# Six terms of a piecewise linear curve added up by GpSimd, ten by TensorE

## What is computed

```python
h = x @ w1 + b1                       # [3125, 1024] @ [1024, 512]
h = round(h * 256) / 256
y = interp(h, X, Y)                   # X: 33 knots from -4 to 4, Y: exact GELU there
y = where(h > 4, h, where(h < -4, 0, y))
y = round(y * 256) / 256
out = round((y @ w2 + b2) * 256) / 256
x = x + out                           # x is normalised before w1
```

## Time and profile before

| | |
|---|---|
| median of 3 runs | 3742.73 us (3742.1 to 3743.62) |
| the profiled execution, its own time | 3739.34 us |
| its span, first to last instruction | 3737.7 us |
| busy in the span: PE | 3444.8 us (92%) |
| busy in the span: DVE | 2799.8 us (75%) |
| busy in the span: ACT | 1582.1 us (42%) |
| busy in the span: POOL | 924.0 us (25%) |

### The profile page before, as it was taken

The page is one execution under the profiler, slowest core; times in us unless marked ns, Lnnn a source line. Parts: engine busy times, 40 slices in busy tenths (PEclk is TensorE's granted clock), DMA queues, the critical chain, the costliest instruction groups (busy, mean ns, idle before and its releaser), DMA issues. The chain is left out here.

```text
span 3737.7 us, 52878 instructions
## 1 busy us (share of the span) xinstructions
PE 3444.8 (92%) x17197; PEld 2842.2 (76%) x17197; DVE 2799.8 (75%) x6375; ACT 1582.1 (42%) x2646; POOL 924.0 (25%) x564
## 2 busy tenths in 40 slices
PE   6899999979999968991999999999999999699998
PEld 5678888658888847771888888888888888577776
DVE  4577677667777744333988989889889898688886
ACT  2011111121111102111777777777777777354454
POOL 1266671057766775660000000000000000000000
PEclk8999999989999989995999999999999999899999
DMA  7833322334444433323011110110110110322221
GB/s 264 350 50 66 66 51 65 104 90 89 89 88 88 88 76 75 47 43 106 23 45 39 28 45 25 42 45 22 45 45 23 45 37 14 112 74 82 82 71 50
DMA packets 234863, 269.87 MB, mean 72 GB/s; under 512 B 177236, under 2 KB 177236, under 8 KB 231642
## 3 DMA queue, kind: packets, MB, share of 16 engines
q1 hardware_dynamic: 57741, 216.14, 19.0%
q0 software_dynamic: 173776, 40.24, 7.5%
q10 hardware_dynamic: 3250, 12.50, 0.9%
HBM read 177.03 MB, written 90.75 MB: 72 GB/s over the span
## 5 line engine op out<-in xcount | busy, mean ns | idle before, releaser
L1194 PE MATMUL G_acc<-values,G_probsT 125*125 125x256 f32 x5000 | 1165.0, 380 | 0.0
L1194 PEld LDWEIGHTS G_acc<-values,G_probsT 125*125 125x125 f32 x5000 | 901.9, 188 | 113.8 <-ACT G_probsT L1057 0.3
L317 POOL DMA_INDIRECT counts<-E_twins_now,E_cells_now x400 | 859.6, 2149 | 389.9 <-issue 252.6
L1030 ACT ACTIVATE G_probs<-G_asrc_row,G_shift 125x625 f32<-125x625 f32 x500 | 409.0, 818 | 384.6 <-PE G_tr L1178 284.2
L1102 DVE TENSOR_TENSOR G_probs<-G_probs,G_low 125x625 f32<-125x625 f32 x500 | 402.3, 805 | 99.9 <-issue 66.0
L1178 PEld LDWEIGHTS G_tr<-ident,G_probs 125*125 125x125 f32 x2500 | 339.5, 189 | 180.2 <-DVE G_probs L1104 160.6
L1178 PE MATMUL G_tr<-ident,G_probs 125*125 125x125 f32 x2500 | 369.7, 279 | 108.1 <-DVE G_probs L1104 103.4
L1104 DVE SCALAR_TENSOR_TENSOR G_probs<-G_probs,G_count 125x625 f32<-125x625 f32 x500 | 405.2, 810 | 17.3
L1035 ACT ACTIVATE G_low<-G_asrc_row,G_low_shift 125x625 f32<-125x625 f32 x500 | 407.5, 815 | 22.9 <-DVE G_probs L1102 22.6
L218 PE MATMUL V_v_ps<-V_w,V_xT 128*125 128x512 f32 x1200 | 281.4, 397 | 43.7 <-DVE V_xT L242 43.7
L218 PEld LDWEIGHTS V_v_ps<-V_w,V_xT 128*125 128x125 f32 x1200 | 224.2, 187 | 100.9 <-DVE V_xT L242 44.1
(11 more groups left out here) (169 smaller groups left out, 3943.1 us busy)
## 6 DMA issues: line engine op xcount, KB each, us to landing
counts<-K_zeros POOLq DMA_DIRECT2D x50, 763.5 KB, 8.3
G_count<-counts SPq DMA_DIRECT2D x25, 1367.2 KB
xnT<-K_xT_whole SPq DMA_DIRECT2D x25, 500.0 KB
Q_xT_whole<-xnT SPq DMA_DIRECT2D x25, 500.0 KB
V_xT_whole<-xnT SPq DMA_DIRECT2D x25, 500.0 KB
E_row<-edge_keys ACTq DMA_DIRECT2D x25, 488.3 KB
E_row<-edge_keys SPq DMA_DIRECT2D x25, 488.3 KB
K_rows<-in_x SPq DMA_DIRECT2D x25, 448.0 KB
```

The source lines that it names most:

```text
L317: nc.gpsimd.indirect_dma_start(out=counts_cells, out_offset=bass.IndirectOffsetOnAxis(ap=self.cells_now[:, slot, c:c + 1], axis=0), in_=se ...
L1030: nc.scalar.activation(probs[:, u % 4, :], asrc_row[:, h, s:s + UW], ACT.Exp, bias=shift[:, sl, h:h + 1]).then_inc(high_ready, 1)
L1194: m = nc.tensor.matmul(acc[0:T, h * C:(h + 1) * C], probsT[:, u % 2, b, :], values[:, t, h * C:(h + 1) * C], start=(t == 0), stop=(t == NT ...
```

## The change

The last six terms go to POOL, and PE keeps ten: PE_TERMS is 10 and FOLDED is range(10, 16). POOL makes each term with one instruction, max(m, knot) * 2 * kink, which is the old term times two plus the constant 2 * kink * knot. DVE takes the six constants off with its first instruction on `halves`, and then signals `halves_ready`. POOL adds its six terms one by one to `halves` and signals `folded_in`, for which DVE now waits before it joins `halves` and `even_ps`.

```diff
-    KN, PE_TERMS = len(KINKS), 14
+    KN, PE_TERMS = len(KINKS), 10
...
+        @block.gpsimd
+        def _(pool):
+            chain = Chain(pool, fold)
+
+            def body(g, n):
+                pool.wait_ge(size_ready, g + 1)
+                pool.sem_inc(seen, 1)
+                for n, i in enumerate(FOLDED):
+                    chain.step(nc.gpsimd.tensor_scalar(folded[:, n, :], magnitude[:, :], KNOTS[i], 2 * KINKS[i], ALU.max, ALU.mult))
+                pool.wait_ge(halves_ready, g + 1)
+                for n, i in enumerate(FOLDED):
+                    chain.settle()
+                    ins = nc.gpsimd.tensor_tensor(halves[:, :], halves[:, :], folded[:, n, :], ALU.add)
+                    if i < KN - 1:
+                        chain.step(ins)
+                ins.then_inc(folded_in, 1)
+            over_tiles(pool, body, chain=chain, steps=2 * len(FOLDED) - 1, **TILES)
...
             def second_half():
-                chain.step(nc.vector.tensor_scalar(halves[:, :], hid[:, :], -4.0, -4.0, ALU.max, ALU.add))
-                for n, i in enumerate(FOLDED):
-                    chain.step(nc.vector.tensor_scalar(folded[:, n, :], magnitude[:, :], -KNOTS[i], 0.0, ALU.add, ALU.max))
-                chain.settle()
-                chain.step(nc.vector.scalar_tensor_tensor(out=halves[:, :], in0=hid[:, :], scalar=4.0, in1=halves[:, :],
-                                                          op0=ALU.max, op1=ALU.add))
-                for n, i in enumerate(FOLDED):
-                    chain.settle()
-                    chain.step(nc.vector.scalar_tensor_tensor(out=halves[:, :], in0=folded[:, n, :], scalar=2 * KINKS[i],
-                                                              in1=halves[:, :], op0=ALU.mult, op1=ALU.add))
+                chain.step(nc.vector.tensor_scalar(halves[:, :], hid[:, :], -4.0, -4.0 - sum(2 * KINKS[i] * KNOTS[i] for i in FOLDED),
+                                                   ALU.max, ALU.add))
+                chain.settle()
+                nc.vector.scalar_tensor_tensor(out=halves[:, :], in0=hid[:, :], scalar=4.0, in1=halves[:, :],
+                                               op0=ALU.max, op1=ALU.add).then_inc(halves_ready, 1)
...
                 dve.wait_ge(even_done, g + 1)
+                dve.wait_ge(folded_in, g + 1)
```

More of the change, by code:

```diff
@@ L1232, in feed_forward @@
     fed_done, fed_free = sem("fed_done"), sem("fed_free")
+    halves_ready, folded_in, fold, seen = sem("halves_ready"), sem("folded_in"), sem("fold"), sem("seen")
     fed_fixed, out_ready, out_stored, out_free = sem("fed_fixed"), sem("out_ready"), sem("out_stored"), sem("out_free")
@@ L1426, in body @@
                     second_half()
-            over_tiles(dve, body, chain=chain, steps=1 + LN_STEPS + 1 + 4 + 2 * len(FOLDED), **TILES)
+            over_tiles(dve, body, chain=chain, steps=1 + LN_STEPS + 1 + 3, **TILES)
             finish(NT - 1, NT - 1)
```

## The result

The changed kernel takes 3906.61 us (median of 4 runs, 3903.05 to 3911.07) where the kernel before takes 3742.41 (4 runs): the ratio is 1.044, with a 95% interval of 1.0422 to 1.0458. It is slower by 164 us. The forecast was 3837, with a range of 3722 to 3895: the sign was right, the size was not.

A forecast was written before the change was run, and what follows sets the result against it. PE bounds at 19.73 us a tile, DVE close behind. With POOL and DVE taking turns, 16.43 + 7.2 = 23.6 us a tile: 90 us over 23 tiles, +4 for first and last, so 3742.73 + 94 = 3837; range 3722 to 3895.

The forecast's parts named there:

- PE's part: Feed-forward terms on PE: eight of 28 matmuls go, 1.86 us, leaving PE's tile at 17.87 us.
- DVE's part: DVE in the feed-forward: two L1368 and two L1374 go, 2.13 us, leaving 15.63 us of work a tile.
- The 16.43 us of a free DVE: DVE's feed-forward tile without holding: 15.63 us of work, 0.16 for statistics, 0.64 waiting for geluT.
- the point of 3.3 us of loss: DVE in each feed-forward tile: it can lose 19.73 - 16.43 = 3.3 us before the kernel is slower.
- PE's price of a term: Feed-forward terms on PE: 0.232 us a matmul, 0.464 a term.
- POOL's one-input instruction: POOL's max-and-times on 125x512, six a tile: 0.64 us each, between 0.53 and 0.76.
- The addition: POOL's addition of two tensors on 125x512, six a tile: 1.12 us each, between 0.94 and 1.40.
- The twelve: POOL's six one-input instructions and six additions in each feed-forward tile: 10.6 us, with ends 8.8 and 13.0.
- the third rival: POOL's twelve instructions themselves slow, 1.3 us and more on average, so the folded_in wait comes late; 3950 us, chance 0.05.
- sum with turns: Third rival's feed-forward tile with POOL and DVE taking turns: 16.43 + 15.6 - 3.4 = 28.6 us, over +200.
- The turn-taking: POOL and two-input DVE instructions on SBUF block each other: 7.2 us lost a tile, +94 us, chance 0.60.
- what doesn't fit under the cover holds DVE: POOL's time beyond 3.4 us beside DVE instructions needing one SBUF tensor holds DVE: 10.6 - 3.4 = 7.2 us a tile.

The follow-up runs named there:

- side: Changed kernel, but POOL does four max-and-times and six additions a tile on its own tiles, nobody waits, six terms left out; 3741.5 us, ratio 1.0003.
- act5n: act6n with 11 terms on PE and five on POOL; 3715.8 us, ratio 0.992.
- alone: Changed kernel plus a block ahead of the feed-forward where POOL runs one-input and two-input instructions with every other engine idle; 3943.34 us.
- act6: Changed kernel, but ACT makes the six terms and POOL only subtracts them from halves; 3757.05 us, ratio 1.005.
- madd: Changed kernel with times-and-add in place of max-and-times in POOL's six one-input instructions, the maximum left out; 3805.97 us, ratio 1.0163.
- four: Changed kernel with 12 terms on PE and four on POOL; 3755.07 us, ratio 1.0038.
- act6n: act6 with the feed-forward layer norm's eight Newton instructions written with one input tensor; 3719.53 us, ratio 0.9935.

## Why the prediction was wrong

**PE's part and DVE's part** were right. The 16.43 us of a free DVE, with its 2.13 us less, are confirmed by four kernels in the table, and so is the point of 3.3 us of loss at which the gain is gone: side loses 3.36 and comes out at 1.0003. PE's price of a term is confirmed by act5n, where PE bounds: 18.33 us by that price, 18.41 measured.

**The step that failed is POOL's one-input instruction**, "I take 0.64, the middle". The change's max-and-times takes 1.93 to 1.95 us with every other engine idle, three times as much. The bounds of 0.53 and 0.76 came from MEMSET and AFFINE_SELECT, which are other programs on POOL; the run alone shows that even the same kind of instruction takes 0.62 or 1.95 by its pair of operations. The addition, taken as 1.12, takes 1.26, and 1.34 from start to start. The twelve were to be 8.8 to 13.0 us and are 20.7 (3503.28 to 3523.93).

**With that the case changes**, from the forecast to the third rival, which the prediction gave 0.05 because "the rows of POOL speak against it". It was to decide as soon as the twelve take over 15.3 us, and `size_ready` to the join is 20.96 (3503.09 to 3524.05). Side by side, the rival's own account is: `gelu_ready` comes at 1.5 + 20.9 + 1.14 = 23.5 us after the product's start and PE is free at 16.05, 7.5 earlier, so the tile is 17.87 + 7.5 = 25.4. It is 26.13, and 0.67 of the difference is the transposes, 1.11 us instead of the 0.44 of the earlier trace rows: PE now stands still for some 7 us ahead of them, and the granted clock of the tiles is 0.84 in the mean where it was 1.00. The prediction had put 0.2 us on that. The price it gave this rival, 3950, came from its sum with turns, 28.6 us a tile, and was too high by 43.

**The turn-taking** was right for POOL's additions and wrong for its one-input instructions. The traces of side, act6 and madd show two-input DVE instructions held to the end of a POOL addition, Newton columns too, as the forecast said and no row of before had shown. The Trainium skill, "SBUF — State Buffer", section "Who interferes with whom", had said so for a GpSimd instruction that reads SBUF; for the additions the trace agrees (0.22 us became 1.23). For POOL's max-and-times it doesn't: it reads SBUF too and runs for 1.93 us, and of eight Newton steps inside such instructions six keep their 0.22 and 0.16 and two lose 0.36 and 0.35, those that begin just behind its start (the rows of the changed kernel above). There the measurement decides, and the forecast's rule "what doesn't fit under the cover holds DVE" overcounts: for madd it gives 24.3 us where 22.09 is measured. In the changed kernel it hardly matters, since six slow one-input instructions push the additions to where DVE has nothing left.

So the sign was right by luck: it came from a mechanism that costs 1.1 us a tile here, within the 8.0 us that DVE waits. What made the kernel slower is the time that POOL's twelve instructions take, one behind the other, with DVE waiting for the last. Three kernels show it: alone has the long instruction with nobody to hold it up, side works POOL much the same (two max-and-times fewer) without the wait and takes 3741.5 instead of 3906.6, and madd keeps the wait and shortens the six instructions and takes 3806.0. By madd, with instructions near the lengths that the prediction took, the kernel is 62 us slower than before, where the forecast's sum with these lengths gives 110: the holding that it overcounts.

**The range** left the third rival out on the strength of three rows of other instructions. The upper end for an instruction that no row shows was set at 1.4 times the lower one (0.76 and 0.53); the measured length is 2.5 times that upper end.

## What to carry to other kernels

- Work handed to an idle engine has to be priced by that very instruction, its operations included, in a block where nothing else runs. Here one pair of operations costs three times another, and the idle engine became the longest way through the tile.
- Give POOL the additions and leave the making of the terms to an engine that makes them quickly, and count which DVE instructions with two SBUF inputs lie beside each addition, and the wide one-input ones (L154 and the roundings here). A small one is held as long as a large one, so a chain of two-input column steps is the worst neighbour; written with one input tensor it is not held.
- A helper that is just hidden has a cliff behind it: with the terms made by ACT and the Newton steps on one input tensor, five terms for POOL gave -29 us, six -25 and seven +11, each against its own runs of the kernel before.

## What was not expected of the hardware

- POOL's tensor_scalar on 125x512 f32 takes 0.62 us for times-and-add and add-and-times, 1.49 to 1.50 for a single times, add or max, and 1.92 to 1.96 for max-and-times, times-and-min, times-and-max, add-and-max and add-and-add. A copy takes 0.61, an addition of two tensors 1.26. Times-and-add with zero is 0.62 where times alone is 1.50.
- A POOL addition holds a one-column, two-input DVE instruction from 0.22 to 1.23 us; the same arithmetic with one input tensor keeps its 0.27 us (100 of 100, 81 of them begun inside a subtraction of the kernel act6n).
- POOL's max-and-times runs for 1.93 us and holds a two-input DVE instruction only where that begins near its start, and by 0.41 us at most. In the tiles between 3300 and 3850 us of the changed kernel the held ones begin 0.03 to 0.12 us behind the start of a max-and-times (one at 0.25) and the Newton steps among them end 0.62 to 0.63 behind it; those that begin at 0.66 or later keep their lengths. In the kernel four the first L148 begins 0.26 behind and ends 0.62 behind. It looks as if POOL took what the two share only for the first 0.6 us; no kernel was made for it.
